# Group statistics by one fp32 product each instead of two, with two more VectorE instructions ahead of each product

## The reference

```
def _gn(v, G=32, eps=1e-05):
    g = v.reshape(B_, H_, W_, G, C_ // G)
    m = jnp.mean(g, axis=(1, 2, 4), keepdims=True)
    s = jnp.var(g, axis=(1, 2, 4), keepdims=True)
    return ((g - m) / jnp.sqrt(s + eps)).reshape(v.shape)

bias = x @ bias_w.T + bias_b
xf = jnp.fft.rfftn(x.reshape(B, H, W, 4, 96), axes=(1, 2), norm='ortho')
r1 = relu(xr @ w1[0] - xi @ w1[1] + b1[0]);  i1 = relu(xr @ w1[1] + xi @ w1[0] + b1[1])
r2 = r1 @ w2[0] - i1 @ w2[1] + b2[0];        i2 = r2 @ w2[1] + i1 @ w2[0] + b2[1]
out = jnp.fft.irfftn(r2 + 1j * i2, s=(H, W), axes=(1, 2), norm='ortho')
return x + out.reshape(B, H, W, C) + bias
```

## Time and profile before

| | |
|---|---|
| median of three runs | 442.46 us (442.2 to 443.78) |
| the profiled execution | 442.63 us, of which the span from first to last instruction is 440.8 us |
| mean granted TensorE clock | 0.965 of full speed |
| PE busy / PEld busy | 401.7 us (91%) / 356.2 us (81%) |
| DVE, ACT, POOL busy | 315.6 (72%), 225.6 (51%), 84.4 us (19%) |
| DMA | mean 75 GB/s; 32.00 MB by the kernel's queue, 1.11 MB by the queue that fetches instructions |

### The profile page before, as it was taken

How to read it: one execution, slowest core, us unless ns; L and a number is a source line. 1 busy time by engine, 2 the same in 40 slices (tenths; PEclk the granted TensorE clock), 3 DMA queues, 4 the chain that set the end, 5 groups by cost and what they waited for, 6 DMA issues and landing times.

```text
span 440.8 us, 19270 instructions
## 1 busy us (share of the span) xinstructions
PE 401.7 (91%) x8530; PEld 356.2 (81%) x8530; DVE 315.6 (72%) x768; ACT 225.6 (51%) x504; POOL 84.4 (19%) x72
## 2 busy tenths in 40 slices
PE   4429969998999999999999999999999899995996
PEld 4427859987898989988898989888898789883894
DVE  3684986777668686768668686868767676869424
ACT  2542577426653476426662566438652576436320
POOL 0000100630009000630027000710036000880000
PEclk9857969999999999999999999999999999999899
DMA  7770000053001700053001700161003500130004
GB/s 218 205 233 1 4 1 3 27 177 126 3 5 37 288 2 5 27 181 121 3 5 71 256 3 4 39 232 58 5 3 128 198 3 4 39 146 1 4 4 144
DMA packets 12567, 33.24 MB, mean 75 GB/s; under 512 B 4994, under 2 KB 6692, under 8 KB 12484
## 3 DMA queue, kind: packets, MB, share of 16 engines
q1 hardware_dynamic: 12484, 32.00, 20.8%
HBM read 16.26 MB, written 12.58 MB: 65 GB/s over the span
## 4 chain that ended last, share of the span: by engine, by line
PE 82%; DVE 9%; ACT 4%; issue 4%; DMA 1%; DVEq 0%; SPq 0%; ACTq 0%
PE bank L552 82%; DVE r L1066 2%; DVE rsum L1059 2%; DVE z L991 1%; DMA x_sb<-in_x 1%; DVE y L991 1%; ACT yraw L867 1%; ACT r L897 1%; ACT junk L875 1%; ACT z L907 1%; ACT biasw L901 1%; DVE g L1218 0%; DVE o_sb L1082 0%; ACT w2s L901 0%; ACT junk L878 0%
## 5 line engine op out<-in xcount | busy, mean ns | idle before, releaser
L552 PE MATMUL bank<-biasw,y 128*64 128x384 f16 x1152 | 112.8, 341 | 0.0
L552 PEld LDWEIGHTS bank<-biasw,y 128*64 128x64 f16 x1152 | 94.2, 196 | 3.1 <-DVE rsum L1059 0.3
L552 PE MATMUL bank<-w2s,rho 128*64 128x96 f16 x3072 | 85.0, 207 | 0.2 <-issue 0.2
L552 PEld LDWEIGHTS bank<-w2s,rho 128*64 128x64 f16 x3072 | 80.1, 109 | 4.4 <-issue 2.9
L853 POOL TENSOR_TENSOR x_sb<-x_sb,added 128x384 f32<-128x384 f32 x56 | 74.6, 1368 | 0.0
L907 ACT ACTIVATE z<-bank 128x384 f16<-128x384 f32 x72 | 35.2, 489 | 67.1 <-PE bank L552 66.5
L552 PE MATMUL bank<-tab,x_sb 128*128 128x128 f32 x384 | 53.5, 295 | 10.0 <-DMA x_sb<-in_x 6.2
L552 PE MATMUL bank<-w1R,y 128*128 128x192 f16 (+3 forms) x768 | 59.8, 228 | 3.1 <-issue 2.6
L552 PEld LDWEIGHTS bank<-tab,x_sb 128*128 128x128 f32 x384 | 49.2, 204 | 13.5 <-issue 7.0
L991 DVE SCALAR_TENSOR_TENSOR z<-bank,z 128x384 f16<-128x384 f32 x72 | 40.0, 557 | 28.1 <-ACT z L907 27.8
L851 POOL TENSOR_TENSOR x_sb<-x_sb,added 128x384 f32<-128x384 f32 x8 | 8.1, 1006 | 259.7 <-DVE yraw L1047 231.1
(11 more groups left out here) (104 smaller groups left out, 433.0 us busy)
## 6 DMA issues: line engine op xcount, KB each, us to landing
x_sb<-in_x SPq DMA_DIRECT2D x16, 768.0 KB, 7.1
out<-o_sb SPq DMA_DIRECT2D x14, 768.0 KB, 3.8
y<-y SPq DMA_DIRECT2D x24, 128.0 KB, 2.7
out<-o_sb SPq DMA_DIRECT2D x8, 192.0 KB, 2.1
tab<-in_tab SPq DMA_DIRECT2D x1, 672.0 KB, 6.1
o_sb<-in_bias_wt SPq DMA_DIRECT2D x4, 144.0 KB, 2.9
b1s<-in_b1h SPq DMA_DIRECT2D x1, 384.0 KB, 5.2
tab<-in_tab SPq DMA_DIRECT2D x1, 291.5 KB, 3.0
```

The costliest lines, as they stand in the source:

```text
L552: return nc.tensor.matmul(o, lhsT, rhs, start=start, stop=stop, **kw)
```

## The change

The two matrices become one, `groups` = `own` + `block3` (their nonzero places do not meet). So that one product gives both kinds of group, the operand must hold, in each fourth partition and for each tile, the sum over the three tiles, and in the other partitions what it held before. A new function `shared` writes this operand with two VectorE instructions: it multiplies the last column by the mask of the fourth partitions, and then makes operand = value x mask of the others + that column, into `mean_in` or `var_in`. It is called behind the sum in `channel_means` and in `moments`. The step numbers grow by two behind each call. The second load of the table is 126 columns (63 KB of 291.5 KB) smaller.

```diff
-for ... in (("width", 256), ("own", 128), ("block3", 128), ("const", 64), ...):
+for ... in (("width", 256), ("groups", 128), ("fourth", 2), ("const", 64), ...):
...
+    fourth = np.arange(128)[:, None] % 4 == 3
+    put("groups", own + block3)
+    put("fourth", np.concatenate([fourth, ~fourth], axis=1))
...
-        MEANS, MOMENTS, VAR_READ, CENTRED = 4, 15, 16, 23
-        NSTEP = 23
+        MEANS, MOMENTS, VAR_READ, CENTRED = 6, 19, 20, 27
+        NSTEP = 27
...
             def group_mean(src, at):
-                mm(y_bank[0][:, at:at + NT], own, src[:, 0:NT], True, False)
-                return mm(y_bank[0][:, at:at + NT], block3, src[:, NT:NT + 1].to_broadcast([128, NT]), False, True)
+                return mm(y_bank[0][:, at:at + NT], groups, src[:, :], True, True)
...
-                group_mean(mc, 0).then_inc(mean_prod, 1)
+                group_mean(mean_in, 0).then_inc(mean_prod, 1)
...
-                group_mean(qv, 8).then_inc(var_prod, 1)
+                group_mean(var_in, 8).then_inc(var_prod, 1)
...
+            def shared(b, k, src, out):
+                stat(b, k)
+                step(nc.vector.tensor_scalar(src[:, NT:NT + 1], src[:, NT:NT + 1], fourth[:, 0:1], None, ALU.mult))
+                stat(b, k + 1)
+                step(nc.vector.scalar_tensor_tensor(out=out[:, :], in0=src[:, 0:NT], scalar=fourth[:, 1:2],
+                                                    in1=src[:, NT:NT + 1].to_broadcast([128, NT]), op0=ALU.mult, op1=ALU.add))
...
                 step(nc.vector.tensor_reduce(mc[:, NT:NT + 1], mc[:, 0:NT], AX.X, ALU.add))
+                shared(b, 4, mc, mean_in)
...
                 step(nc.vector.tensor_reduce(qv[:, NT:NT + 1], qv[:, 0:NT], AX.X, ALU.add))
+                shared(b, 17, qv, var_in)
```

More of the change, by code:

```diff
@@ L165 @@
 TABW = TAB16W = 0
-for _name, _wide in (("width", 256), ("own", 128), ("block3", 128), ("const", 64), ("sign", 3), ("coef", 4), ("impulse", 128), ("row0", 128)):
+for _name, _wide in (("width", 256), ("groups", 128), ("fourth", 2), ("const", 64), ("sign", 3), ("coef", 4), ("impulse", 128), ("row0", 128)):
     TAB[_name] = (TABW, TABW + _wide)
@@ L191, in constants @@
     put("inv_low", G_EVAC * inv.astype(np.float16))
-    put("own", own)
-    put("block3", block3)
+    fourth = np.arange(128)[:, None] % 4 == 3
+    put("groups", own + block3)
+    put("fourth", np.concatenate([fourth, ~fourth], axis=1))
     put("const", np.broadcast_to(const, (128, 64)))
@@ L257, in spectral_block_kernel @@
         mc = sb("mc", [128, NT + 1])
+        mean_in = sb("mean_in", [128, NT])
+        var_in = sb("var_in", [128, NT])
         mg = sb("mg", [128, NT])
@@ L392, in spectral_block_kernel @@
         inv, inv_low = (T(name).rearrange("k s (a m) -> k s a m", a=2) for name in ("inv", "inv_low"))
-        own = T("own")
-        block3 = T("block3")
+        groups = T("groups")
+        fourth = T("fourth")
         const = T("const")
@@ L1002, in channel_means @@
                 step(nc.vector.tensor_reduce(mc[:, NT:NT + 1], mc[:, 0:NT], AX.X, ALU.add))
+                shared(b, 4, mc, mean_in)
                 step(nc.vector.tensor_tensor(xs1[:, :, :, :], bc(mc), constb, ALU.mult))
-                stat(b, 5)
+                stat(b, 7)
                 step(nc.vector.tensor_tensor(xs1[:, :, :, :], xcols(), xs1[:, :, :, :], ALU.subtract))
-                stat(b, 6)
+                stat(b, 8)
                 step(nc.vector.tensor_tensor(xs2[:, :, :, :], xs1[:, :, :, :], xs1[:, :, :, :], ALU.mult))
-                stat(b, 7)
+                stat(b, 9)
                 step(nc.vector.tensor_reduce(sX[:, :], xs2[:, :, :, :], AX.XY, ALU.add))
             def moments(b):
-                stat(b, 8)
+                stat(b, 10)
                 dve.wait_ge(y_sq, 2 * NT * (b + 1))
@@ L1018, in moments @@
                 step(nc.vector.tensor_copy(mg[:, :], y_bank[0][:, 0:NT]))
-                stat(b, 9)
+                stat(b, 11)
                 step(nc.vector.scalar_tensor_tensor(out=sX[:, :], in0=sumsq[:, 1, :], scalar=2.0, in1=sX[:, :], op0=ALU.mult, op1=ALU.add))
-                stat(b, 11)
+                stat(b, 13)
                 step(nc.vector.tensor_tensor(dev[:, :], mc[:, 0:NT], mg[:, :], ALU.subtract))
-                stat(b, 12)
+                stat(b, 14)
                 step(nc.vector.tensor_tensor(dev[:, :], dev[:, :], dev[:, :], ALU.mult))
-                stat(b, 13)
+                stat(b, 15)
                 step(nc.vector.scalar_tensor_tensor(out=qv[:, 0:NT], in0=sX[:, :], scalar=1.0 / PIX, in1=dev[:, :], op0=ALU.mult, op1=ALU.add))
-                stat(b, 14)
+                stat(b, 16)
                 step(nc.vector.tensor_reduce(qv[:, NT:NT + 1], qv[:, 0:NT], AX.X, ALU.add))
+                shared(b, 17, qv, var_in)
             def scales(b):
@@ L1035, in scales @@
                 step(nc.vector.reciprocal(rstd[:, :], std_t[:, :]))
-                stat(b, 17)
+                stat(b, 21)
                 step(nc.vector.tensor_tensor(newton[:, :], rstd[:, :], rstd[:, :], ALU.mult))
-                stat(b, 18)
+                stat(b, 22)
                 step(nc.vector.tensor_tensor(newton[:, :], newton[:, :], var[:, :], ALU.mult))
-                stat(b, 19)
+                stat(b, 23)
                 step(nc.vector.tensor_scalar(newton[:, :], newton[:, :], -0.5, 1.5, ALU.mult, ALU.add))
-                stat(b, 20)
+                stat(b, 24)
                 step(nc.vector.scalar_tensor_tensor(out=rstd[:, :], in0=rstd[:, :], scalar=Y_SCALE, in1=newton[:, :], op0=ALU.mult, op1=ALU.mult))
                 step(nc.vector.tensor_tensor(xs1[:, :, :, :], bc(mg), constb, ALU.mult))
-                stat(b, 22)
+                stat(b, 26)
                 step(nc.vector.tensor_tensor(xcols(), xcols(), xs1[:, :, :, :], ALU.subtract))
```

## The result

| | before | changed |
|---|---|---|
| median of ten runs each, in turn on one chip | 442.41 us (440.62 to 443.87) | 439.34 us (438.89 to 441.13) |
| ratio | | 0.994, 95% interval 0.9919 to 0.9961 |
| the profiled execution (span) | 442.63 us (440.8) | 439.48 us (437.7) |
| PE busy / DVE busy | 401.7 / 315.6 us | 397.1 / 322.1 us |

The kernel became 0.6% faster, 3.1 us by the medians and 3.15 by the profiled executions. The forecast was 439.6.

What follows compares the result with a forecast made beforehand. TensorE, 82% of the chain, was taken as the bound, with VectorE's added work covered. Products -3.1 us and start +0.2 made -2.9, giving 439.6 us; range 437.2 to 442.8.

Steps and rivals of the forecast that it cites:

- TensorE's saving: Group products of images 1 to 7: two fewer matmul records each, 0.22 us per product, 14 x 0.22 = 3.1 us.
- VectorE's time: Images 0 to 6: added instructions take 0.39 us per pair, 0.78 per image, 5.5 over seven, costed at nothing.
- cover of the reading of the variance: VectorE, behind the two g_low after the variance: they end at 373.75, the reading could start at 373.98; cover 0.23 us.
- The covers as a list: Statistics of each image: slack said to hide VectorE's added work, at mean, g_low(0), moments, variance and the variance's reading.
- the variance product: TensorE's product in moments: operand ready at 372.81, TensorE comes at 373.55; cover 0.74 us.
- the mean product: TensorE's product in channel_means: operand ready at 368.69, TensorE comes at 369.54; cover 0.85 us.
- the two of under 0.3 us: Covers on VectorE in the statistics: 0.29 us behind g_low(0) and 0.23 us behind g_low(2).
- The start: Before image 1, VectorE's pair in moments is not covered: var about 0.2 us later, bounds -0.1 to 0.39.
- the mechanism that was named: At the start, var waits behind the low half of w1R on VectorE, no longer for TensorE; about 0.2 us later.
- The fetch rival: Stops of TensorE for instruction fetch change: 436.7 to 445.2; chance 0.17 of going wrong by over 1 us (440.7 to 444).
- excess: Time from image 1's mean to image 7's beyond six times the undisturbed period, 48.70 us; 2.9 us before the change.
- Slower, or nothing done: VectorE becomes bound in the statistics: 445.4 up to 448, chance 0.06; product still cut into four records: 442.7, chance 0.03.

Runs made afterwards that it cites:

- e1: Changed kernel with a second fp32 matmul of the same matrix and operand behind each group product, into columns nobody reads; 442.11 us, ratio 1.0005 to the kernel before.
- e2: Kernel before with only the first fp32 matmul of each group product, block 3's sum left out, no new VectorE instructions; 439.63 us, ratio 0.9938.
- e3: Changed kernel with the pair of VectorE instructions in the moments done twice; 441.59 us, ratio 0.9998 to the kernel before.
- e10: Changed kernel with the VectorE pair in the moments done twice and 64 small matmuls at the start; 439.56 us, ratio 0.9951 to the kernel before.
- e6: Changed kernel with 64 small f16 matmuls (128 TensorE instructions) in TensorE's idle time at the start; 437.51 us, ratio 0.9902 to the kernel before.
- e12: Changed kernel with the mask of the others first, so one instruction waits for the sum, and 64 small matmuls at the start; 437.18 us, ratio 0.9890.
- e8: Changed kernel with the mask of the others first, so only the pair's second instruction waits for the sum; 440.16 us, ratio 0.9955 to the kernel before.

## Why the prediction was right

- **TensorE's saving: right.** The distance of the records that go was the price: a product took 0.54 and takes 0.32 us, the period fell by 0.44 to 0.45 (48.70 to 48.25) as in 14 x 0.22 = 3.1, and e1 gave it all back. By the Trainium skill, "TensorE: Matmul & The Clock Gate", section "Back-to-back issue gap", which the prediction cites for 25 ns per matmul of few columns, it would have been 0.05 us per product; the trace has 0.22.
- **VectorE's time: the step was mis-sized, the conclusion held.** I priced a pair at 0.39 us from instructions whose scalar is a constant (L1174) or that I took to be like L1026, which has one too. The new ones read their scalar from memory, one per partition: 0.21 and 0.22 us instead of 0.15 and 0.16, with starts 0.25 us apart instead of 0.19. The pair moves what is behind it by 0.50: at the start the low half of `w1R` begins 20.32 - 19.74 = 0.58 us behind the sum L1039, where it was 0.08. So the cover of the reading of the variance is some 0.12 us, not 0.23. It was enough: e2, without the pairs, has the same ratio within the interval and the same period, 48.25. In the kernel before the same group reads:

```profile
20.81 0.16 DVE L1028 TENSOR_REDUCE qv<-qv 128x1 f32<-128x3 f32 x1
20.89 1.01 DVE L991 SCALAR_TENSOR_TENSOR w1R<-o_sb,s,w1R 128x768 f16<-128x768 f32 x1
```

- **The covers as a list: incomplete.** I named the variance product (0.74 us; 370.38 - 369.72 = 0.66 in the trace) and the mean product (0.85; 366.33 - 365.61 = 0.72) as the wide ones and the two of under 0.3 us as the thin ones. `g_low(0)` ends at 367.51, 0.19 us ahead of `c2_bias(3)` at 367.70, where I forecast 0.29. The list has no line for `g_low(1)` and `c2_bias(4)`, and that is where one more pair first costs TensorE time (e3, e10).
- **The start: right in the group, open for the whole.** +0.2 was forecast; 0.24 is the trace's distance from L1027 to `var`, by the mechanism that was named. That the end of the kernel pays it is not shown: between the two executions the clock at the start moved more than that.
- **The fetch rival: real, and hardly moved by this change.** The excess went from 2.9 us to 2.6. The ends that I gave, 436.7 and 445.2, stand for an excess of 0 and of 8.5 us; the traces of the changed kernel's TensorE work show 0.5 (e6, e12) to 4.8 us (e8). Placing alone moved the ratio by 0.4% and the median by 1.8 us (e6), and one period of e10, 51.07 us, holds a stop of 1.5 us and more behind it that I have not taken apart.
- **The closeness of the number: partly luck.** The products are worth 2.7 us in the six periods, as forecast. The rest of the 3.15 us of the profiled executions I did not forecast so: 0.3 from shorter stops, 0.19 up to the mean of image 1 (where 0.2 was to be lost) and -0.06 behind the mean of image 7 (where two more products were to save 0.44). These differences nearly cancel.
- **Slower, or nothing done:** neither happened; the records are two, and no `c2_bias` waits for `g_low` in the changed kernel.

## What to carry to other kernels

Price a small matmul at the distance from one record's start to the next in the same run of the program, not at its length and not at its columns: here three columns cost 0.11 us with their weights. Moving such work to an engine with idle time is free only up to the thinnest cover; here that was the cover of `g_low(1)`, which only stands behind the added work on VectorE and reads nothing of it. So list every instruction behind the added one on its engine with who waits for it, and measure one more than you add. When a kernel of one long instruction stream stops for "issue" at a fixed step of instruction numbers, shift the stream by part of a block before judging changes of under 1%.

## What the runs showed of the hardware

- A VectorE instruction of one to three columns takes 0.15 to 0.17 us with constants (0.15 for L1186 on one column, 0.17 for L1010 on three) and 0.21 to 0.22 us when its scalar is read per partition (L998, L1000), and a dependent successor starts 0.25 instead of 0.19 us later.
- TensorE's instructions come in blocks of 256. Where it had to stop for one, it went on 2.2 to 2.8 us behind the start of a packet of the instruction queue (41 stops in fourteen traces). A block whose fetch falls into a burst of stores and loads (91.8% of the DMA engines busy) came up to 1.8 us late.
